# Attention with a split maximum: half differences, merged value columns and units shared with the score banks

## The reference

```python
x = x + xattn(_layernorm(x), ctx_1024, ctx_1024, _lenS2, ...)   # x: 1 x 2048 x 256, ctx: 1 x 1601 x 256
x = x + ffn(_layernorm(x), gate_w, w1, w2, w3)                  # 8 experts, the best 2 of each row

# xattn: 16 heads of width 64
q_in, k_in, v_in = layer_norm(query), layer_norm(key), layer_norm(value)
q, k, v = q_in @ Wq + bq, k_in @ Wk + bk, v_in @ Wv + bv        # split into heads
q, k = rope(q), rope(k)
scores = einsum('bhqd,bhkd->bhqk', q, k) / 8
scores = where(arange(sk) < length, scores, -inf)
out = softmax(scores) @ v
return out.reshape(...) @ Wo + bo
```

## Time and profile before

| | us |
|---|---|
| median of 3 runs | 1426.77 |
| lowest, highest | 1425.2, 1431.77 |
| profiled execution, its own time | 1433.12 |
| its span, first to last instruction | 1431.2 |
| PE busy in the span | 1116.6 |
| DVE busy | 1055.5 |
| ACT busy | 651.2 |
| POOL busy | 690.2 |

### The profile page before, as it was taken

The page is one execution under the profiler, slowest core; times in us unless marked ns, Lnnn a source line. Parts: engine busy times, 40 slices in busy tenths (PEclk is TensorE's granted clock), DMA queues, the critical chain, the costliest instruction groups (busy, mean ns, idle before and its releaser), DMA issues. The chain is left out here.

```text
span 1431.2 us, 31650 instructions
## 1 busy us (share of the span) xinstructions
PE 1116.6 (78%) x10244; PEld 728.6 (51%) x10407; DVE 1055.5 (74%) x1793; ACT 651.2 (46%) x1196; POOL 690.2 (48%) x496
## 2 busy tenths in 40 slices
PE   1659798888889889888888898997677616999863
PEld 0324465555556556555555555664466503666531
DVE  6647997998999799799799889997457522444324
ACT  3525555555555455555555555564455401322210
POOL 0054754854774574575476466554456561000142
PEclk9758999999999999999999999999989858999985
DMA  7041123121221312312312142174187121111223
GB/s 237 23 116 31 37 53 80 42 57 53 63 49 36 87 35 47 92 34 54 78 43 46 34 97 49 26 231 130 45 316 246 60 101 57 53 55 51 73 84 107
DMA packets 98004, 114.75 MB, mean 80 GB/s; under 512 B 44957, under 2 KB 78046, under 8 KB 97630
## 3 DMA queue, kind: packets, MB, share of 16 engines
q1 hardware_dynamic: 87310, 86.13, 22.4%
q10 hardware_dynamic: 7504, 18.51, 3.9%
q0 software_dynamic: 3072, 8.39, 1.8%
HBM read 43.61 MB, written 30.02 MB: 51 GB/s over the span
## 5 line engine op out<-in xcount | busy, mean ns | idle before, releaser
L798 DVE TENSOR_REDUCE part_max<-mx 128x1 f32<-128x427 f32 x768 | 420.0, 593 | 86.1 <-PE mx L581 85.2
L706 ACT ACTIVATE prob<-sc 128x512 f32<-128x512 f32 x640 | 349.7, 595 | 240.3 <-PE sc L569 236.6
L885 POOL TENSOR_TENSOR prob_lo<-prob 128x1024 bf16<-128x1024 f32 x128 | 251.6, 1965 | 271.2 <-ACT prob L706 271.2
L581 PE MATMUL mx<-K,Q 128*128 128x427 bf16 x768 | 244.2, 359 | 85.3 <-DVE part_max L798 54.5
L607 PE MATMUL pv<-VV,prob 128*128 128x129 bf16 x2560 | 278.1, 225 | 8.8 <-POOL prob_lo L885 8.6
L609 PE MATMUL pv<-VV,prob_lo 128*128 128x65 bf16 x2560 | 269.0, 197 | 0.0
L569 PE MATMUL sc<-Q,K 65*128 65x512 bf16 x640 | 253.9, 397 | 9.6 <-issue 4.4
L607 PEld LDWEIGHTS pv<-VV,prob 128*128 128x128 bf16 x2560 | 239.8, 100 | 41.9 <-POOL prob_lo L885 9.2
L810 DVE TENSOR_TENSOR prob_lo<-prob 128x1024 bf16<-128x1024 f32 x192 | 253.6, 1321 | 5.8 <-ACT prob L706 5.6
L609 PEld LDWEIGHTS pv<-VV,prob_lo 128*128 128x128 bf16 x2560 | 234.4, 100 | 27.6 <-issue 3.7
L568 PE MATMUL sc<-Q,K 128*128 128x512 bf16 x519 | 206.0, 397 | 0.7 <-ACT prob L706 0.7
(11 more groups left out here) (185 smaller groups left out, 1865.1 us busy)
## 6 DMA issues: line engine op xcount, KB each, us to landing
we<-in_w_exp ACTq DMA_DIRECT2D x16, 768.0 KB, 5.6
q32s<-q SPq DMA_DIRECT2D x128, 64.0 KB, 2.0
Q<-next_q_hi SPq DMA_DIRECT2D x32, 256.0 KB, 3.6
attention_out<-o_out SPq DMA_DIRECT2D x64, 128.0 KB, 2.0
o_in<-attention_out SPq DMA_DIRECT2D x16, 512.0 KB, 4.8
VV<-next_v SPq DMA_DIRECT2D x16, 322.5 KB, 3.7
q32s<-q SPq DMA_DIRECT2D x128, 40.0 KB, 1.9
K<-next_k_hi SPq DMA_DIRECT2D x32, 160.0 KB, 3.4
```

Of the source, the lines that this page charges most:

```text
L581: ins = pe.matmul(mx[:, bank, 0:pl.width], Q1[a][:, c * QC + qt * P:c * QC + (qt + 1) * P], K1[a][:, k0:k0 + pl.width], start=True, stop=True)
L706: act.activation(prob[:, s % PRING, j, :], sc[n % 2][:], ACT.Exp, scale=HD ** -0.5).then_inc(exp_done, 1)
L798: dve.tensor_reduce(part_max[:, b_ % 2, qt, h:h + 1], mx[:, pl.part_banks(qt, h)[0]:pl.part_banks(qt, h)[-1] + 1, 0:pl.width], mybir.AxisL ...
L885: pool.tensor_tensor(prob_lo[:, s % PRING, 0:g, :], prob[:, s % PRING, 0:g, :], hi_half(prob[:, s % PRING, 0:g, :])[:, :, 1::2], ALU.subtr ...
```

## The change

1. The maximum. `next_kd` is the difference of the keys' second and first half. For each 128 queries PE makes the scores of the first half of the keys (`mx_first`, 64 rows, partitions 0 to 63) and the scores of the difference (`mx_diff`, partitions 64 to 127), 2 matmuls of 320 columns each. ACT takes `Relu` of the difference into `above` (`rise`), and DVE adds the first half and takes the maximum in one instruction (`tensor_tensor_reduce`). There are 4 parts in a block in the place of 12, each in one slot: groups 4 (of two blocks ahead), 0, 1 and 2. `mx_first` and `mx_diff` take four banks, once each.
2. Values. Output of 4 query tiles is 65 columns each in one bank: a third matmul adds the product with the values' low half onto the same columns. DVE scales the result straight out of PSUM (`output`); `copy_out` on ACT and the two POOL instructions are gone.
3. Units. They are 3 slots apart (slots 6, 9, ... 36) and use the two `sc` banks in turn with the score tiles; the bank `pj` is gone. `cosines` reads the bank and adds the bias itself. `q32` and `q32s` are two deep, `by_cos` three. Invalid keys are replaced in `prepare` (`KHI`, `KLO`), so L775, L778 and L780 become one `turn`. POOL gets `key_rise`, SP one more DMA in `load_k`, which stands in slot 34; the first part that reads it stands in slot 34 too.
4. Order. PE: `max_row`, scores, `project`, `times_v`, part. ACT: `max_row`, exps, hooks, `rise`. DVE: `low`, `output`, cosines, turn or `v_lo`, part, `max_column`. `max_row` moves from group 3 to group 4.
5. `wo_hi` and `wo_lo` are made in `prepare`.

```diff
+        self.first_part = self.groups - 6
+        self.hook_step = (BLOCKS * self.groups - self.groups - 5) // (self.units - 1)
...
     def parts_of(self, s):
         i, m = divmod(s, self.groups)
-        ahead, at = (2, m - self.groups + 2) if m >= self.groups - 2 else (1, m + 2)
-        return [(i + ahead, n // len(self.parts), n % len(self.parts)) for n in self.parts_at[at]]
+        return [(i + 1 + (self.first_part + qt < 0), qt) for qt in range(QT) if (self.first_part + qt) % self.groups == m]
...
     def row_block(self, s):
-        return i + 1 if m == self.groups - 2 else None
+        return i + 1 if m == self.groups - 1 else None
     def hook_slot(self, k):
-        return self.groups * (1 + k // 2) + (0, 2)[k % 2]
+        return self.groups + 1 + self.hook_step * k
...
+                dve.wait_ge(lo_made, C_TURNS)
+                for h, part in enumerate((CHI, CLO)):
+                    ins = dve.tensor_copy(first_key[:, h, :], part[:, :, 0])
+                ins.then_inc(first_made, 1)
+                dve.wait_ge(first_made, 1)
+                for h, (part, whole) in enumerate(((CHI, KHI), (CLO, KLO))):
+                    for d in range(DT):
+                        dve.scalar_tensor_tensor(out=whole[:, d, :], in0=invalid[:], scalar=first_key[:, h, d:d + 1],
+                                                 in1=part[:, d, :], op0=ALU.mult, op1=ALU.add)
...
         sc = [pb(f"sc{i}", [P, QC]) for i in range(2)]
         pv = pb("pv", [P, 2, 512])
-        mx = pb("mx", [P, 3, 512])
-        pj = pb("pj", [P, 512])
+        mx_first = pb("mx_first", [P, 2, 512])
+        mx_diff = pb("mx_diff", [P, 2, 512])
...
@@ PE, project @@
+                            place = pl.unit_place(u)
+                            need(pe, sc_read, pair, pl.turns, place - 1 - pl.turns, least)
+                            before = pl.unit_before(place)
+                            if before is not None:
+                                need(pe, unit_taken, pair, pl.units, before + 1, least)
+                        pj = sc[place % 2]
...
@@ PE, part @@
-                        need(pe, part_read, p, BLOCKS * pl.block_parts, pl.block_parts * b_ + len(pl.parts) * qt + h + 1)
-                        for bank, k0 in zip(pl.part_banks(qt, h), pl.parts[h]):
-                            ins = pe.matmul(mx[:, bank, 0:pl.width], Q1[a][:, c * QC + qt * P:c * QC + (qt + 1) * P],
-                                            K1[a][:, k0:k0 + pl.width], start=True, stop=True)
+                        need(pe, above_made, p, BLOCKS * QT, n)
+                        need(pe, part_read, p, BLOCKS * QT, n)
+                        cols = slice(c * QC + qt * P, c * QC + (qt + 1) * P)
+                        for h in range(2):
+                            keys = slice(h * pl.kc, (h + 1) * pl.kc)
+                            pe.matmul(mx_diff[:, h, 0:pl.kc], Q1[a][HD:P, cols], KD[a][HD:P, keys], start=True, stop=True)
+                            ins = pe.matmul(mx_first[:, h, 0:pl.kc], Q1[a][0:HD, cols], K1[a][0:HD, keys], start=True, stop=True)
                         ins.then_inc(part_ready, 1)
...
@@ PE, times_v @@
-                                at = (qt % 2) * VW
-                                pe.matmul(pv[:, qt // 2, at:at + VW], hi[:, 2 * qt * P + 1:2 * (qt + 1) * P:2], VV[a][:, t, :],
-                                          start=t == 0 and qt % 2 == 0, stop=False, skip_group_check=True)
-                                ins = pe.matmul(pv[:, qt // 2, at + HD:at + VW], prob_lo[:, s % PRING, j, qt * P:(qt + 1) * P],
-                                                VV[a][:, t, HD:VW], start=False, stop=t == pl.kt - 1, skip_group_check=True)
+                                out = pv[:, i % 2, qt * (HD + 1):(qt + 1) * (HD + 1)]
+                                hi_q = hi[:, 2 * qt * P + 1:2 * (qt + 1) * P:2]
+                                pe.matmul(out, hi_q, VV[a][:, t, HD:VW], start=t == 0 and qt == 0, stop=False, skip_group_check=True)
+                                pe.matmul(out[:, 0:HD], hi_q, VV[a][:, t, 0:HD], start=False, stop=False, skip_group_check=True)
+                                ins = pe.matmul(out, prob_lo[:, s % PRING, j, qt * P:(qt + 1) * P], VV[a][:, t, HD:VW],
+                                                start=False, stop=t == pl.kt - 1, skip_group_check=True)
...
@@ ACT @@
+                    def rise(p, b_, qt):
+                        n = QT * b_ + qt
+                        need(act, part_ready, p, BLOCKS * QT, n + 1)
+                        need(act, part_read, p, BLOCKS * QT, n - 1)
+                        act.activation(above[:, n % 2, :, 0:pl.kc], mx_diff[:, :, 0:pl.kc], ACT.Relu).then_inc(above_made, 1)
...
@@ DVE @@
-                        dve.tensor_tensor(by_cos[:, 0:n], q32[:, u % 4, 0:n], (ropeq, ropek)[kind][:, 0, cols], ALU.mult).then_inc(cos_done, 1)
+                        dve.scalar_tensor_tensor(out=by_cos[:, u % 3, 0:n], in0=unit_bank(pair, u)[:, 0:n], scalar=bqk[:, kind:kind + 1],
+                                                 in1=(ropeq, ropek)[kind][:, 0, cols], op0=ALU.add, op1=ALU.mult).then_inc(unit_taken, 1)
...
+                    def part(p, b_, qt):
+                        n = QT * b_ + qt
+                        need(dve, above_made, p, BLOCKS * QT, n + 1)
+                        dve.sem_inc(above_seen, 1)
+                        dve.tensor_tensor_reduce(above[:, n % 2, :, 0:pl.kc], mx_first[:, :, 0:pl.kc], above[:, n % 2, :, 0:pl.kc],
+                                                 1.0, -3e38, ALU.add, ALU.max, part_max[:, b_ % 2, qt:qt + 1]).then_inc(part_read, 1)
...
+                    def output(p, i):
+                        need(dve, pv_done, p, BLOCKS * pl.groups, pl.groups * (i + 1) + PRING)
+                        sums = pv[:, i % 2, 0:QT * (HD + 1)].rearrange("p (t v) -> p t v", v=HD + 1)
+                        dve.reciprocal(rden[:, i % 2, :], sums[:, :, HD]).then_inc(rden_made, 1)
+                        need(dve, o_stored[i % 2], p, 16 * BLOCKS // 2, 16 * (i // 2 + 1))
+                        need(dve, rden_made, p, BLOCKS, i + 1)
+                        dve.tensor_tensor(o_out[:, i % 2, :, :], sums[:, :, 0:HD],
+                                          rden[:, i % 2, :].unsqueeze(2).to_broadcast([P, QT, HD]), ALU.mult).then_inc(o_made, 1)
...
@@ POOL @@
+                    def key_rise(pair, least=0):
+                        need(pool, qk_hi_made, pair, QK_UNITS, QK_UNITS, least)
+                        for a in range(2):
+                            need(pool, k_loaded[a], pair, 64, 0, least)
+                        pool.tensor_tensor(next_kd[:, 0:2 * pl.kc], next_hi[1][:, 2 * pl.kc:4 * pl.kc], next_hi[1][:, 0:2 * pl.kc],
+                                           ALU.subtract).then_inc(kd_made, 1)
...
@@ SP, load_k @@
-                        need(sp, qk_lo_made, pair, QK_UNITS, 8, 0 if isinstance(pair, int) else 1)
+                        need(sp, kd_made, pair, 1, 1, 0 if isinstance(pair, int) else 1)
...
+                        sp.dma_start(KD[a][HD:P, 0:n // 2], next_kd[r, 0:n // 2]).then_inc(k_loaded[a], 16)
```

374 lines of the change are left out of this document (185 added, 189 removed).

## The result

The changed kernel takes **1583.24 us** (median; 1580.88 to 1584.77) where the kernel before took 1429.1 beside it: a ratio of **1.108, 95% interval 1.1045 to 1.1114**. It is slower by a tenth; the forecast of 1412 and the whole range to 1478 missed it. The profiled execution has a span of 1580.7 us against 1431.2.

The account below looks back on a forecast made before the run. DVE was taken to bound loaded pairs, PE blocks without units. Seven loaded pairs -18.2 us, last pair +1.2, before the loop +3: -14, from 1433.1 to 1419; the median lying 6.3 lower, 1412 us, range 1338 to 1478 (8 in 10).

Parts of the forecast that it names:

- What bounds the kernel: In loaded pairs DVE, busy 106.15 of 117.6 us; in blocks without units PE, 10.5 of 10.73 us.
- The durations: Maximum's instructions: rise on ACT 0.72 us, reduce on DVE 0.82, couples of matmuls 0.14 apart, array change 0.16.
- rival 2: The array's halves do not work side by side: slot 2.48 us, block 12.0, 1468 us in all; chance 0.23.
- The ring: A part's way through PE, ACT and DVE until PE may issue the next: 2.13 us, slot 2.2, block 10.9.
- The hand-offs: Passing a part from PE to ACT, ACT to DVE and DVE to PE: 0.05 us each.
- The column: DVE's column of maxima after group 2's part, ahead of PE's transposes: 0.05 + 0.17 + 0.05 us.
- Values: Third value matmul starts within 0.03 us, at most 3 us a pair; DVE's output, about 0.6 us, hides in group 1.
- Units: Units in the score banks cost a pair 15.9 us of PE's slots plus 4.2 for turns on DVE.
- The keys: Slot 34's part waits for the next pair's keys: 6.2 us a pair, plus 1.7 of slow clock.
- Before the loop: Added passes in prepare +7.4 us, earlier units about -7, the first four parts +2.8: together +3.
- 3: Rival: tensor_tensor_reduce costs more than a maximum by length; 0.15 us more gives 1450 us, two passes 1580; chance 0.12.
- 4: Rival: DVE's time is no limit of the loaded pairs, so a pair takes 126.7 us, 1495 in all; chance 0.03.

Follow-up runs that it names:

- before_cos: The kernel before with cosines made on DVE from PSUM, bias added on the way, one unit earlier; 0.981 of the kernel before.
- values_alone: The kernel before with only the new value products and output (third matmul, reciprocal and product on DVE); 1.015 of the kernel before.
- col_keys: The changed kernel with the column of maxima written by a tensor_reduce and units 14/5 slots apart; 1.010 of the kernel before.
- col_reduce: The changed kernel with the column of maxima written by a tensor_reduce, not a tensor_copy; 1495.0 us, 1.045 of the kernel before.
- keys_early: The changed kernel with units 14/5 slots apart, the last in slot 34 instead of 36; 1515.7 us, 1.060 of the kernel before.
- before_even: before_cos with units 14/5 slots apart, in place of two a block; 1.034 of the kernel before.

## Why the prediction was wrong, point by point

**What bounds the kernel**: right. The loaded pairs paid for DVE's held products; before_cos takes the hold from one kind of them and gains 5 us a pair.

**The durations**: right. `rise` 0.70 (0.72 forecast), the reduce 0.82 (0.82), and the halves of the array side by side: starts at the same time, the second couple 0.13 behind, no rival 2. A change between whole and half array costs some 0.1 us from start to start (0.13 from the last value matmul where 0.03 is usual, 0.23 to the next score tile where 0.13 is), not 0.16. The ring in the last pair, one turn of it:

```profile
1103.47 0.29 PE L629 MATMUL mx_diff<-KD,Q 64*128 64x320 bf16 x1 [0.19 <-DVE part_max L842]
1103.47 0.31 PE L630 MATMUL mx_first<-K,Q 64*128 64x320 bf16 x1
1103.60 0.29 PE L629 MATMUL mx_diff<-KD,Q 64*128 64x320 bf16 x1
1103.62 0.30 PE L630 MATMUL mx_first<-K,Q 64*128 64x320 bf16 x1
...
1103.95 0.70 ACT L760 ACTIVATE above<-mx_diff 128x640 f32<-128x640 f32 x1 [0.67 <-PE mx_first L630]
...
1104.84 0.82 DVE L842 CUSTOM_DVE_ANT_1 above<-mx_first,above 128x640 f32<-128x640 f32 x1 [0.30 <-ACT above L760]
1105.59 0.08 DVE L842 DVE_READ_ACCUMULATOR2_ANT part_max<- 128x1 f32 x1
...
1105.82 0.29 PE L629 MATMUL mx_diff<-KD,Q 64*128 64x320 bf16 x1 [0.19 <-DVE part_max L842]
```

**The hand-offs** failed: three of 0.05, from one row. PE to ACT is 0.03 (1103.92 to 1103.95), but ACT to DVE 0.19 (1104.65 to 1104.84), and DVE to PE 0.15 behind the reading of the accumulator. The ring is 2.35 us, not 2.13, and a slot 2.35, not 2.2. A plain block of the last pair is 1111.15 - 1099.50 = 11.65 us, not 10.9 (starts of L765), as the column and the stretch behind it have such hand-offs too: 0.75 x 8 = 6 us a pair.

**The column** failed, by the most. "0.05 + 0.17 + 0.05" took its duration from a `tensor_reduce` for an instruction of another kind. That was a wrong nearest row: the kind decides whether it waits for POOL. In the rows stood the sign of it, cosines at 1561 ns for 512 columns, which I put down to both engines reading SBUF without asking what else POOL would hold. The runs showed 1.83 us in 7 of 8 blocks for the 0.17, 12.5 us a pair.

**Values**: right for the third matmul, 0.03 us. That DVE's output hides holds in the changed kernel's ring (in the last pair it ends at 1106.38 us, and the next reduce starts at 1107.19, released by ACT); in the kernel before it didn't, and values_alone lost 2.0 us a pair.

**Units**: 20.1 us a pair forecast, 116.6 - 8 x 11.63 = 23.6 in col_keys. From 300 to 1000 us PE waited there 13.0 + 5.6 us for exponentials, 0.3 a time, which was in the sum at 0.5 a unit, and 5.8 + 4.4 for DVE, which was set to nothing under a cover that did not hold: some 1.9 us a pair. The rest of the 3.5 stays open.

**The keys**: right in kind. The wait was 4.4 instead of 6.2, the slow clock longer. From the same pair as the cast above, in the columns of the earlier trace rows:

```profile
507.50:510.00 2.50, 1.56 (x27) 1.10 (x28) 0.95 (x2) 1.67 (x3) 1.64 (x2) 1.00 0.00 0
510.00:512.50 2.50, 0.00 (x0) 0.00 (x0) 0.48 (x1) 0.00 (x0) 0.00 (x0) 0.78 0.83 188
512.50:515.00 2.50, 1.44 (x6) 0.41 (x7) 0.00 (x0) 0.68 (x1) 0.00 (x0) 0.50 0.21 48
515.00:517.50 2.50, 2.50 (x29) 1.78 (x29) 1.57 (x3) 1.22 (x3) 0.00 (x0) 0.50 0.00 0
```

The granted clock falls to 0.50 (1.2 of 2.4 GHz) within the hole and stays there through a stretch of full work. 6.2 + 1.7 were forecast, 8.0 is the difference of col_reduce and col_keys. As the units' spacing changed with it, and keys_early gave 10.2, the close match is luck.

**Before the loop**: +3 forecast, +12.5 measured (the first row of the maximum, 107.09 to 119.54 us). The units start 13.5 us later instead of 7.4 (four passes of 1.9 are 7.6, a third pass for the cosines 1.9; the other 4 I haven't taken apart), take 4.7 less instead of 7, and the first parts 3.7 more instead of 2.8.

**The sum** of the misses: the column 12.5 x 7 = 88, the ring 6 x 7 = 42, the units 3.5 x 7 = 25, before the loop 9.5, the last pair 4 (its seven blocks 5.0 us longer in col_keys, 1.2 forecast): some 168. What lies behind the last column is 3 us shorter (420.4 to 417.1), which leaves 165. From 1419 to the profiled 1582.7 it is 164. The units' term is what is left of a pair when the others are taken off, so the sum closes by construction there.

**The rivals**: 2 came to a block of 12.0 us, near to the 11.65, by a mechanism that wasn't there. 3 had the accumulator's second instruction at 0.17; it is 0.08; its form of two passes came to 1580 us, beside the measured 1583 by chance alone, as the reduce took one pass, 0.82 us. 4 was wrong in its ground (DVE's time is a limit). None was the one that decided: an instruction of one engine held by another's.

**Still open**: whether ACT's 0.19 us to DVE comes from the wait and the count on `above_seen` in front of the reduce wasn't tried; which of shared banks and key features costs the 4.6 us a pair; what the even slots cost before_even beyond the key wait; and what the new maximum is worth alone, with old slots on both sides.

## What to carry to other kernels

For a moved or replaced instruction take the price from a row of the same kind with the same places of its operands, and look at what the other engine of a shared port does at that time. Compare its longest row with its shortest: a group with a mean of 1.43 us and a least of 0.17 is not slow, it is held. And before a part is passed round three engines over one set of banks, count every hand-off by a row of its own pair of engines; 0.22 us in a ring of 2.13, paid in every block, was more than the 14 us of gain forecast.
